# A fused two-attention kernel on one core: order of the probability transposes, the expert attention product and two products u

## What is computed

```python
gv = _gate(x, Wsel_v)
v = jnp.einsum('bsd,bhse,hedp->bhsp', x, gv, Wv)
att = jax.nn.softmax(jnp.einsum('bhsp,bhtp->bhst', q, k) / np.sqrt(P), axis=-1)
o = jnp.einsum('bhst,bhtp->bhsp', att, v)
go = _gate(x, Wsel_o)
return jnp.einsum('bhsp,bhse,hepd->bsd', o, go, Wo)
```

## Time and profile before

| what | value |
|---|---|
| median of 3 runs | 3403.58 us (3402.18 to 3407.0) |
| profiled execution, span | 3401.4 us |
| outside the span, by the median | 2.2 us |
| PE busy | 3233.1 us, 95% |
| DVE busy | 2439.7 us, 72% |
| ACT busy | 1961.5 us, 58% |
| POOL busy | 1441.9 us, 42% |
| DMA, HBM read and written | 262.74 MB, 31.98 MB |
| mean granted clock of PE | 0.995 of full |

### The profile page before, as it was taken

The page is one execution under the profiler, slowest core; times in us unless marked ns, Lnnn a source line. Parts: engine busy times, 40 slices in busy tenths (PEclk is TensorE's granted clock), DMA queues, the critical chain, the costliest instruction groups (busy, mean ns, idle before and its releaser), DMA issues.

```text
span 3401.4 us, 64468 instructions
## 1 busy us (share of the span) xinstructions
PE 3233.1 (95%) x18240; PEld 2378.9 (70%) x18240; DVE 2439.7 (72%) x4708; ACT 1961.5 (58%) x4509; POOL 1441.9 (42%) x1215
## 2 busy tenths in 40 slices
PE   1699999999999999999999999999999999997998
PEld 1577777777777777777777777777777777775765
DVE  6577777777777777777777777777777777775554
ACT  2466666656666666666666666666666666664121
POOL 4144355445443454345543554434534543442212
PEclk9999999999999999999999999999999999999999
DMA  5223333334233333233233332333332433333221
GB/s 165 76 71 87 95 90 85 77 76 109 76 84 87 84 98 81 75 100 96 69 87 76 96 98 77 76 104 81 84 87 68 114 81 75 84 75 110 72 83 62
DMA packets 115937, 295.18 MB, mean 87 GB/s; under 512 B 33856, under 2 KB 54592, under 8 KB 99264
## 3 DMA queue, kind: packets, MB, share of 16 engines
q1 hardware_dynamic: 115904, 294.78, 32.9%
HBM read 262.74 MB, written 31.98 MB: 87 GB/s over the span
## 4 chain that ended last, share of the span: by engine, by line
PE 85%; issue 6%; DVE 5%; ACT 3%; DMA 1%; POOL 0%; ACTq 0%; SPq 0%; DVEq 0%; POOLq 0%
PE bank L673 27%; PE bank L799 22%; PE bank L718 9%; PE bank L773 7%; PE bank L688 5%; PE bank L905 4%; PE bank L897 3%; PE bank L693 3%; PE bank L745 2%; PE bank L754 2%; ACT probs L957 2%; DVE uf L1239 1%; DVE oo L1232 1%; PE bank L694 1%; ACT pt_e L977 1%
## 5 line engine op out<-in xcount | busy, mean ns | idle before, releaser
L573 POOL TENSOR_TENSOR u_l<-uf,u_h 128x512 fp32r<-128x512 f32 x512 | 716.1, 1409 | 722.6 <-ACT u_h L1041 722.4
L1136 DVE TENSOR_REDUCE nmax<-bank 128x1 f32<-128x512 f32 (+3 forms) x1024 | 551.8, 579 | 305.0 <-PE bank L688 297.8
L673 PE MATMUL bank<-wv_h,xx 128*128 128x512 f32 x2048 | 755.0, 410 | 7.1 <-DVE vm L1157 7.1
L957 ACT ACTIVATE probs<-bank,nmax 128x512 f32<-128x512 f32 (+3 forms) x1024 | 590.7, 610 | 253.2 <-DVE nmax L1136 253.1
L1041 ACT ACTIVATE u_h<-uf 128x512 fp32r<-128x512 f32 x512 | 321.7, 632 | 696.9 <-DVE uf L1239 683.6
L673 PEld LDWEIGHTS bank<-wv_h,xx 128*128 128x128 f32 x2048 | 386.0, 188 | 155.8 <-issue 59.6
L718 PEld LDWEIGHTS bank<-ident_sb,probs 128*128 128x128 f32 x3328 | 388.3, 141 | 106.4 <-issue 51.3
L718 PE MATMUL bank<-ident_sb,probs 128*128 128x128 f32 x3328 | 451.3, 274 | 1.6 <-ACT stackT L1032 0.9
L569 POOL TENSOR_TENSOR v_sb<-v_next,zero_hb 128x512 f32<-128x512 f32 x64 | 74.2, 1160 | 891.9 <-PE bank L773 877.4
L799 PE MATMUL bank<-u_h,wo_h 128*128 128x512 f32 x1024 | 427.1, 417 | 5.0 <-ACT u_h L1041 3.2
L1239 DVE TENSOR_TENSOR uf<-oo,go 128x512 f32<-128x512 f32 x512 | 416.2, 823 | 8.8 <-POOL u_l L573 6.6
(11 more groups left out here) (141 smaller groups left out, 5164.2 us busy)
## 6 DMA issues: line engine op xcount, KB each, us to landing
go<-go_d SPq DMA_DIRECT2D x256, 512.0 KB, 6.5
xx<-xs_d SPq DMA_DIRECT2D x128, 512.0 KB, 3.5
oo<-scale_d SPq DMA_DIRECT2D x128, 128.0 KB, 2.9
a_d<-a_out SPq DMA_DIRECT2D x128, 128.0 KB, 2.3
pt_c<-in_x SPq DMA_DIRECT2D x16, 512.0 KB, 4.7
st<-in_wv SPq DMA_DIRECT2D x16, 512.0 KB, 5.8
st<-in_wo SPq DMA_DIRECT2D x16, 512.0 KB, 7.2
go_d<-go_turned SPq DMA_DIRECT2D x256, 8.0 KB
```

The lines of the kernel that those rows point to most:

```text
L573: nc.gpsimd.tensor_tensor(u_l[:, e % 2], uf[:, e % 2], u_h.bitcast(f32)[:, e % 2], ALU.subtract).then_inc(ul_done, 1)
L673: last = nc.tensor.matmul(out, lhs, rhs, start=n == 1, stop=n == 3 * len(chunks))
L957: nc.scalar.activation(probs[:, s % 2, j, 0:w], sbank[j][:, 0:w], ACT.Exp, bias=nmax[:, 2 * s + j:2 * s + j + 1], **kw).then_inc(exp_done, 1)
L1136: nc.vector.tensor_reduce(nmax[:, 2 * s + j:2 * s + j + 1], sbank[j][:, 0:w], AX.X, ALU.max, negate=True).then_inc(nmax_ready, 1)
```

## The change

Three things move, and one wait is added.

- PE: `turn(s)` becomes a job of the list, ("TU", s). In steps two to eight it stands where it was, at the end. In the first step it stands ahead of AT: scores(1), P 0 to 3, turn(0), AT.
- ACT: `turned(s)` becomes a job too. In the first step the order is P 0 to 3, EX, turned(0), UH 0; UH 1 moves to the start of step two's jobs, behind the exponentials of unit 2. turned(0) now waits, in bodies other than FIRST, for `w_full` of AT, since AT no longer stands ahead of turn(0).
- DVE: U 1 moves from the end of the first step to step two, behind the maxima of unit 2 and ahead of CH 1.

The arithmetic, the instructions and their number are the same.

```diff
@@ -35,24 +35,24 @@
 BEHIND = ("AT", "AC", "ON", "U", "UH", "UL", "J", "YA")
 AHEAD = ("P", "V", "QK", "ST", "QH", "QL", "SO", "RP", "RS", "PA", "PB", "RA", "PC", "VN", "SQ", "SK", "EX", "CH")
 
-PE_FILL = [[("P", 0), ("P", 1), ("P", 2), ("P", 3), ("AT", 0)],
-           [("AC", 0), ("V", 0)],
-           [("J", 0), ("V", 1), ("J", 1)],
-           [("V", 2), ("J", 2), ("J", 3)],
-           [("V", 3), ("J", 4), ("V", 4)],
-           [("QK", 0), ("J", 5), ("QK", 1)],
-           [("V", 5), ("J", 6), ("V", 6)],
-           [("V", 7), ("ST", 0), ("ST", 1), ("J", 7)]]
-ACT_FILL = [[("P", 0), ("P", 1), ("P", 2), ("P", 3), ("EX", 0), ("UH", 0), ("UH", 1)],
-            [("AC", 0), ("VA", 0), ("PA", 0)],
-            [("UH", 2), ("UH", 3), ("VN", 0)],
-            [("UH", 4), ("UH", 5)],
-            [("UH", 6), ("PB", 0)],
-            [("QH", 0), ("QH", 1), ("UH", 7)],
-            [("SQ", 0), ("SK", 0)],
-            [("SO", 0), ("SO", 1)]]
-DVE_FILL = [[("CH", 0), ("ON", 0), ("U", 0), ("U", 1)],
-            [("CH", 1)],
+PE_FILL = [[("P", 0), ("P", 1), ("P", 2), ("P", 3), ("TU", 0), ("AT", 0)],
+           [("AC", 0), ("V", 0), ("TU", 1)],
+           [("J", 0), ("V", 1), ("J", 1), ("TU", 2)],
+           [("V", 2), ("J", 2), ("J", 3), ("TU", 3)],
+           [("V", 3), ("J", 4), ("V", 4), ("TU", 4)],
+           [("QK", 0), ("J", 5), ("QK", 1), ("TU", 5)],
+           [("V", 5), ("J", 6), ("V", 6), ("TU", 6)],
+           [("V", 7), ("ST", 0), ("ST", 1), ("J", 7), ("TU", 7)]]
+ACT_FILL = [[("P", 0), ("P", 1), ("P", 2), ("P", 3), ("EX", 0), ("TU", 0), ("UH", 0)],
+            [("UH", 1), ("AC", 0), ("VA", 0), ("PA", 0), ("TU", 1)],
+            [("UH", 2), ("UH", 3), ("VN", 0), ("TU", 2)],
+            [("UH", 4), ("UH", 5), ("TU", 3)],
+            [("UH", 6), ("PB", 0), ("TU", 4)],
+            [("QH", 0), ("QH", 1), ("UH", 7), ("TU", 5)],
+            [("SQ", 0), ("SK", 0), ("TU", 6)],
+            [("SO", 0), ("SO", 1), ("TU", 7)]]
+DVE_FILL = [[("CH", 0), ("ON", 0), ("U", 0)],
+            [("U", 1), ("CH", 1)],
             [("U", 2), ("V", 0), ("U", 3)],
             [("V", 1), ("U", 4), ("V", 2), ("U", 5)],
             [("V", 3), ("U", 6)],
@@ -108,10 +108,8 @@
     out = []
     for s in range(SLOTS):
         for j in fill(kind, PE_FILL, s):
-            if j == ("ST", bank):
+            if j == ("ST", bank) or j[0] == "TU":
                 out.append(j)
-        if kind in (FIRST, INNER, LAST):
-            out.append(("turn", s))
     return out
 
 
@@ -712,7 +710,7 @@
                 def turn(s):
 
                     for j in range(2):
-                        o = t_bank(j, ("turn", s))
+                        o = t_bank(j, ("TU", s))
                         pe.wait_ge(exp_done, it * UNITS + 2 * s + j + 1)
                         for c in range(TT if s % 2 == 0 else s // 2 + 1):
                             mm = nc.tensor.transpose(o[:, c * NP:(c + 1) * NP], probs[:, s % 2, j, c * NP:(c + 1) * NP], ident_sb[:])
@@ -759,9 +757,9 @@
 
                     for i in range(2):
                         if kind == TAIL:
-                            pe.wait_ge(t_free[i], t_at(LAST, it, i, ("turn", s)) + 1)
+                            pe.wait_ge(t_free[i], t_at(LAST, it, i, ("TU", s)) + 1)
                         else:
-                            pe.wait_ge(t_free[i], t_at(INNER, it, i, ("turn", s)) + 1 - NT[i])
+                            pe.wait_ge(t_free[i], t_at(INNER, it, i, ("TU", s)) + 1 - NT[i])
 
                 def attend():
 
@@ -810,6 +808,8 @@
                         turn_heads(i)
                     elif name == "ST":
                         turn_stack(i)
+                    elif name == "TU":
+                        turn(i)
                     elif name == "AT":
                         attend()
                     elif name == "AC":
@@ -850,7 +850,6 @@
                         first_scores()
                     for job in fill(kind, PE_FILL, s):
                         do(job)
-                    turn(s)
 
             body(PRO, 0)
             body(FIRST, 0)
...
```

More of the change, by code:

```diff
@@ L867, in _ @@
             for i in range(2):
-                pe.wait_ge(t_free[i], t_at(LAST, PAIRS - 1, i, ("turn", 7)) + 1)
+                pe.wait_ge(t_free[i], t_at(LAST, PAIRS - 1, i, ("TU", 7)) + 1)
             def c_bank(name, at):
@@ L974, in turned @@
                     dst = pt_e if s % 2 == 0 else pt_c
+                    if s == 0 and kind != FIRST:
+                        act.wait_ge(w_full, w_at(kind, it, ("AT", 0))[2] + 1)
                     for j in range(2):
-                        act.wait_ge(t_full[j], t_at(kind, it, j, ("turn", s)) + 1)
+                        act.wait_ge(t_full[j], t_at(kind, it, j, ("TU", s)) + 1)
                         nc.scalar.activation(dst[:, j, 0:m, qt * NP:(qt + 1) * NP], tbank[j][:, 0:m * NP].rearrange("q (c m) -> q c m", m=NP),
@@ L992, in do @@
                         nc.scalar.activation(raw[:, i, :], o[:, 0:NPROJ], ACT.Copy).then_inc(free, 1)
+                    elif name == "TU":
+                        turned(i)
                     elif name == "EX":
@@ L1055, in body @@
                         do(job)
-                    turned(s)
             body(PRO, 0)
```

## The result

| kernel | median | range |
|---|---|---|
| before | 3403.29 us (4 runs) | 3402.18 to 3407.0 |
| after | 3481.64 us (4 runs) | 3478.94 to 3483.49 |

The ratio is 1.0225, with a 95% interval of 1.0213 to 1.0237: 78 us slower. The profiled executions have spans of 3477.1 and 3401.4 us, 75.7 apart, at the same mean granted clock of 0.995.

A forecast was written before the change was run, and what follows sets the result against it. It took TensorE, tied at `mix(3)` to GpSimd's `u_l` 3 through VectorE's chain, as the bound. Per iteration +0.87 +0.77 +0.70 -1.10 -0.02 = +1.22 us; 62 times gives 76, so 3403.6 + 76 = 3479 us, range 3445 to 3498.

The forecast's parts named there:

- What bounds: At `mix(3)`: TensorE already tied to GpSimd's `u_l` 3, slack -0.07 us; the `probs` wait is 0.75 us per iteration.
- The first edit: Transposes ahead of the attention product in step one: product 0.87 us later, the scores after it 0.15 us earlier.
- The bound of up to 0.3 for the neighbouring tilings: Attention product's end ahead of a 64-row tiling: extra cost nothing or up to 0.3 us; taken as the same.
- The second edit: U1 behind the maxima: issued during `u_l` 0, loses 0.77 us; L1185 loses 0.70; CH 1's earlier hold-up of 1.10 goes.
- 1.22 was the sum: VectorE's chain up to the maxima ahead of U2: +0.87, +0.77, +0.70, -1.10, -0.02 rounding, so 1.22 us later.
- The waits: TensorE: `u_l` wait at `mix(3)` 62 times about 1.5 us; step two's `probs` wait 0.2 to 0.4; one appears in step three.
- The total: 62 inner bodies, each 1.22 us longer, make 76 us: 3479; nothing added for first body, last body or tail.
- A: Rival: U1 or L1185 slips past `u_l`, hold-ups partly hidden; 33 to 54 us slower, 3437 to 3458; chance 0.14.
- The argument against A: U1 is issued 0.38 us after `u_l` 0 starts, said to be the same distance as in rows showing the hold-up.
- B: Rival: neither U1 nor CH 1 meets `u_l`, chain -0.23 us per iteration; 14 us faster, 3389; chance 0.06.

The follow-up runs named there:

- v1_act_only: Kernel before with only ScalarE's order changed: step one's two `pt_e` copies ahead of UH0 and UH1, with the added wait for AT; 3404.83 us, ratio 0.9997.
- e1_turn_only: Changed kernel with U1 and UH1 put back beside U0 and UH0, leaving the transposes ahead of the attention product; 3459.2 us, ratio 1.0156.
- e2_u1_only: Changed kernel with TensorE's order put back (attention product, then transposes), ScalarE's and VectorE's lists as changed; 3425.27 us, ratio 1.0061.
- e4_after_narrow: Changed kernel with each `u_l` subtraction on GpSimd made in 16 of 512 columns, output not the reference's; 3353.95 us, ratio 0.9847.
- e3_before_narrow: Kernel before with each `u_l` subtraction on GpSimd made in 16 of 512 columns, output not the reference's; 3389.83 us, ratio 0.9958.

## Why the prediction was right

It said 3479 us (3445 to 3498), slower; it measured 3481.64. Point by point:

- *What bounds.* Confirmed, and by v1_act_only more than by the change itself: `mix(3)` was tied to `u_l` 3 in the kernel before, and a gain of 0.75 ahead of it came to nothing.
- *The first edit, 0.87 later and 0.15 earlier.* In after, the product starts at 5.24 against 4.38 (0.86) and the scores at 8.82 against 8.99 (0.17). The bound of up to 0.3 for the neighbouring tilings was not needed: 1416.55 to 1420.13 is 3.58, against 3.59 before. That part is luck, since no row had this neighbour.
- *The second edit.* U1 took 1.46 (forecast 0.68 + 0.77 = 1.45), L1187 0.98 (0.29 + 0.70 = 0.99), L1184 0.29; the maxima of unit 3 start at 17.69 us of the iteration, against 16.45: 1.24 later, where 1.22 was the sum. The split between the edits is shown by e1_turn_only (55 us for 0.87 x 62 = 54) and e2_u1_only (21 us).
- *The waits.* `probs` in step two: the row of two transposes starts at 1423.74 and the scores at 1424.24, 0.50 behind it, against 0.97 before. The two transposes are 0.11 apart, so without a wait the scores stand 0.22 behind the row's start (as in v1_act_only); the wait was 0.75 and is 0.28, inside the forecast of 0.2 to 0.4. The prediction's working is not clean here: it took 1486.08, the start of the second transpose, as the time at which the scores are due, then took 0.11 off the 0.86 a second time, which gives the right 0.75 (due at 1486.19); its "0.4" for after still goes by the wrong time, and with the right one it is 0.28. For `u_l` it had 62 times 1.5, some 90 us; the view shows 1.31 each and 82.9 us. The lateness was right and the view counts less: the matmul ahead starts at 1433.86, so `mix(3)` was due at 1434.09 and starts 1.48 late, but the idle time is counted from the modelled end of that matmul, 1434.26. The due time, 1496.16 on the clock of before, is inside the 1495.7 to 1496.2 of the prediction. The fifth unit's scores waited 0.42 by the view, 62 times; that a wait appears there was forecast, its size was not.
- *The total.* Median period 47.83 against 46.61, 1.22; the spans are 75.7 apart for 76. I had put nothing on the first, last and tail bodies. From the last projection start to the start of the last matmul of the last product it is 100.7 us against 97.8, of which one inner iteration explains 1.2; the remaining 1.7 I did not trace.
- *The rivals.* A needed U1 or L1187 to slip past `u_l`; over the 62 inner iterations U1 takes 1.45 to 1.47 us and L1187 0.97 to 1.00, so both are caught in each. The argument against A was weaker than it reads: U1 was to be issued 0.38 behind the start of `u_l` 0, which it was, but the rows that show a hold-up have 0.04 (L1182 behind `u_l` 1) and 0.70 (U0 behind `v_sb`), not the same distance. B, a gain once U1 and L1187 meet no `u_l`, is seen in e4_after_narrow: 36 us rather than 14, since there the tie is gone too.

The Trainium skill's rule on the shared port (SBUF — State Buffer, Who interferes with whom), that a VectorE instruction with two SBUF inputs contends with a GpSimd instruction that reads SBUF, is borne out by e3_before_narrow and e4_after_narrow: with the GpSimd instruction at 0.22 us instead of 1.29, the same comparisons take 0.29 at the same place in VectorE's list. (The Trainium skill, same section, keeps one-input work free of it only outside VectorE's 2-port modes, which the prediction leaves out; nothing here turns on that.) What the rows add is the size: a held-up product ends 0.55 us behind the subtraction and a comparison 0.15 us behind it, both some 0.13 less than their 0.68 and 0.29 alone.

## What to carry to other kernels

A wait that the profile counts is not worth its us if the next product is tied to another engine. Look at each later semaphore for the distance between what releases it and the start that it releases, and take a distance equal to the usual latency (0.15 us here) as a tie even where no idle time is shown. Moving work ahead of a product moves everything behind that product on all engines; follow the longest chain to where it meets TensorE again, and then to the next such place: with the tie at `mix(3)` undone, the change still cost 68 us, collected at three others. And where VectorE and GpSimd both do two-input work out of SBUF, as here, an order is also a choice of who meets whom: a VectorE instruction issued 0.04 to 0.5 us behind the start of a subtraction paid 0.7 to 1.1 us.

## What the runs showed that I had not expected

A wait at `mix(3)` costs TensorE about 0.08 us beyond its lateness, since the second matmul of the restarted run follows at 0.31 instead of 0.23 us: 0.07 us of lateness cost 0.16 per iteration (median period 46.45 in e3_before_narrow, 46.61 before). The idle time that the waits view counts is lower still, as it starts at a modelled end: 1.31 us for a start that is 1.48 late, and nothing at all for the 0.28 us in step two. It is therefore a low estimate of what a tie costs.
